# Eight batches of attention and adapters on one core: the loop over the first seven batches written out

## The reference

```python
x = x + attn0(prev=x, self=f)            # 16 heads of 32: q from f, k and v from x, plus one "self" score per row
x = x + softmax((x + e[stage]) @ f.T) @ f # one head over all 512 values
h = relu(x @ W1[lang] + b1[lang])
x = x + norm(x + h @ W2[lang] + b2[lang]) * gamma[lang] + beta[lang]
x = x + (x @ A[r].T) @ B[r].T + lang_embed[r]
```

## Time and profile before

| | before |
|---|---|
| median of three runs | 1429.83 us (1429.33 to 1430.75) |
| span of the profiled execution | 1427.7 us |
| PE busy | 1320.6 us, 92% |
| DVE busy | 930.6 us, 65% |
| ACT busy | 880.7 us, 62% |
| POOL busy | 430.4 us, 30% |
| chain that ended last | PE 61%, ACT 13%, DVE 12%, issue 11%, DMA 1%, POOL 1% |

### The profile page before, as it was taken

One profiled execution on the slowest core, in us unless ns is written; L12 is line 12 of the kernel. 1 busy time (PEld: TensorE's weight loads), 2 busy tenths in 40 slices (PEclk: granted clock), 3 DMA queues, 4 the chain that ended last, 5 costly groups with the idle time before them and its releaser, 6 DMA issues.

```text
span 1427.7 us, 22882 instructions
## 1 busy us (share of the span) xinstructions
PE 1320.6 (92%) x7009; PEld 560.8 (39%) x7009; DVE 930.6 (65%) x1594; ACT 880.7 (62%) x1853; POOL 430.4 (30%) x372
## 2 busy tenths in 40 slices
PE   4799999899998999889998899989999999999995
PEld 1332354324633255332553235432354324533253
DVE  6386458864688546975569654896458864688444
ACT  2398536974378834877448764587536874378731
POOL 5331026310443105331064201651026310443114
PEclk8899999999999999999999999999999999999996
DMA  4213012130120302212021301213012130120200
GB/s 159 70 45 99 1 36 69 38 107 1 53 71 28 99 15 59 62 65 52 31 56 49 115 1 31 74 38 108 1 41 65 45 100 1 54 73 24 69 1 30
DMA packets 62204, 76.26 MB, mean 53 GB/s; under 512 B 14378, under 2 KB 35174, under 8 KB 62062
## 3 DMA queue, kind: packets, MB, share of 16 engines
q1 hardware_dynamic: 62062, 74.54, 18.4%
HBM read 40.81 MB, written 8.40 MB: 34 GB/s over the span
## 4 chain that ended last, share of the span: by engine, by line
PE 61%; ACT 13%; DVE 12%; issue 11%; DMA 1%; POOL 1%; DVEq 0%; ACTq 0%; SPq 0%; POOLq 0%
PE bank L441 22%; PE banks L441 12%; DVE nmx L974 7%; PE bank L1319 7%; PE banks L1303 6%; ACT banks L734 6%; PE bank L1164 5%; ACT big L786 5%; PE banks L1237 3%; PE bank L1266 2%; PE bank L1329 1%; PE bank L1271 1%; PE bank L1293 1%; DVE y L1020 1%; PE bank L1224 1%
## 5 line engine op out<-in xcount | busy, mean ns | idle before, releaser
L734 ACT ACTIVATE banks<-banks,nmx 128x512 f32<-128x512 f32 x512 | 340.5, 671 | 55.8 <-DVE nmx L974 53.1
L974 DVE TENSOR_REDUCE nmx<-banks 128x1 f32<-128x512 f32 x512 | 325.9, 683 | 69.7 <-PE banks L1237 67.9
L786 ACT ACTIVATE big<-banks 128x1024 f32<-128x1024 f32 x256 | 247.9, 1021 | 64.5 <-PE banks L1303 49.7
L441 PE MATMUL bank<-fT,w_hi 128*128 128x512 f16 x768 | 244.0, 379 | 0.8
L1237 PE MATMUL banks<-KQ 97*128 97x512 f16 x512 | 154.1, 382 | 39.5 <-ACT banks L734 36.9
L516 POOL TENSOR_TENSOR big<-x,b2r 128x512 f32<-128x512 f32 x32 | 40.6, 1268 | 438.6 <-DVE x L909 397.5
L1303 PE MATMUL banks<-KQ 98*128 98x512 f16 x512 | 146.7, 396 | 23.5 <-ACT big L786 18.6
L441 PE MATMUL bank<-fT,w_lo 128*128 128x512 f16 x384 | 145.5, 379 | 0.0
L1319 PE MATMUL bank<-big,V 128*32 128x512 f32 x1024 | 142.2, 629 | 0.0
L477 POOL TENSOR_TENSOR half<-qk,ones 128x512 f16<-128x512 f32 x64 | 66.6, 1040 | 240.0 <-ACT qk L716 240.0
L441 PEld LDWEIGHTS bank<-fT,w_hi 128*128 128x128 f16 x768 | 74.7, 97 | 90.9 <-issue 11.9
(11 more groups left out here) (142 smaller groups left out, 1987.6 us busy)
## 6 DMA issues: line engine op xcount, KB each, us to landing
KQ<-half SPq DMA_DIRECT2D x384, 64.0 KB, 2.0
tiles_in<-in_x_dram SPq DMA_DIRECT2D x32, 256.0 KB, 7.1
tiles_in<-in_fside_BxSxS_dram SPq DMA_DIRECT2D x32, 256.0 KB, 2.7
x<-in_x_dram SPq DMA_DIRECT2D x8, 1024.0 KB, 5.4
out_dram<-x SPq DMA_DIRECT2D x32, 256.0 KB, 2.1
w<-in_L_cond_W_dram SPq DMA_DIRECT2D x16, 256.0 KB, 4.6
b2r<-in_L_cond_b_dram SPq DMA_DIRECT2D x8, 256.0 KB, 4.5
gr<-in_L_cond_gamma_dram SPq DMA_DIRECT2D x8, 256.0 KB, 5.3
```

The lines of the kernel that those rows point to most:

```text
L441: mm = eng.matmul(out_ap, pairs[n][0], pairs[n][1], start=(first and n == 0), stop=(last and n == len(pairs) - 1))
L734: ins = eng.activation(bank(step, i)[:, j % 2, :], bank(step, i)[:, j % 2, :], ACT.Exp, bias=nmx[:, t, h:h + 1], accum_out=esum[:, t, h:h ...
L786: eng.activation(big[:, n % 2, 2 * u:2 * u + 2, :], bank(step)[:, :, :], ACT.Exp).then_inc(read(step), 1)
L974: eng.tensor_reduce(nmx[:, t, h:h + 1], bank(step, i)[:, j % 2, :], AX_X, ALU.max, negate=True).then_inc(max_done, 1)
```

## The change

The five loops become Python loops, so each engine gets seven copies of the pass. The loop register, the branch and the instructions that work out counts and addresses go away. The order of the other instructions stays as it was on every engine. All five places of the diff read alike; two of them:

```diff
@@ POOL, L541 @@
-            with eng.Fori(0, B - 1) as i:
+            for i in range(B - 1):
                 add_bo(i)
                 mid(True, True, i)
             add_bo(B - 1)
```

## The result

The changed kernel takes 1403.95 us (median of four runs, 1402.62 to 1405.11) against 1429.58 us: 0.9818 of the time before, with a 95% interval of 0.9806 to 0.983. That is 25.6 us less, where 22.6 were predicted; 1407.2 us was the prediction, 1402.5 to 1411 us its range. Run once more, beside the kernel before on one other chip, it took 1403.04 us against 1430.71: 27.7 us less. The profiled execution took 1404.92 us with a span of 1402.9 us, 24.8 us under that of before.

A forecast was written before the change was run, and what follows sets the result against it. PE was taken as the bound (busy 92%), made to wait behind ACT's branch back. Terms -22.90 + 0.31 + 0 = -22.6 us took the 1427.7 us span to 1405.1, plus 2.1 for the runs' median: 1407.2 us, range 1402.5 to 1411.

The forecast's parts named there:

- Part 1: Start of attention, batches 1 to 6: without the six branches back, late exponential and lower PE clock go, saving 22.90 us.
- Part 2: Branches on PE, DVE, POOL and SP: hidden or already counted in the attention windows, so nothing is added.
- rival C: Start of attention: something else, such as shift rows or SP's loads, is late instead; 1429 to 1430 us, chance 0.05.
- Part 3: Attention: waits by constants add a semaphore instruction, five steps of 0.06 us; pass 0 loses 0.31 us.
- Part 4: Register instructions in layer1 and mid: taken as 0, between 3.5 us gained and 2.1 us lost.
- rival A: Mid: all 0.5 us a pass of DVE's wait at L964 is gained too, giving 1403.7 us; chance 0.09.
- the main case: Whole kernel: the summed terms hold, giving 1405 to 1409.5 us; chance 0.75.
- Part 5: Instruction fetch: seven written-out copies need no more code brought in than the loop does now; cost 0.
- Rival D: Instruction stream falls behind at block ends, 2.7 us a stop; at two a pass 1445 us, slower; chance 0.05.
- Rival B: Start of attention: PE's clock falls all the same, only the late exponential goes; 1417.0 us, chance 0.06.

The follow-up runs named there:

- ACT's loop alone: The changed kernel with only ACT's loop put back, the other four engines written out: 1427.63 us, 0.9971 of the kernel before.
- the request: Kernel before, all five loops kept, each asking for its loop's code ahead of the branch: 1415.00 us; with ACT alone so, others written out: 1408.09 us.
- PE kept at work: Changed kernel with ACT's loop back and 12 extra matmuls on PE while it waits for ACT's first exponential, passes 1 to 6: 1415.05 us.
- both places of ACT's loop: Kernel before, five loops, DVE's loop starting at place 0 of a code block, ACT's at place 0 (1428.21 us) or 64 (1429.43 us).

## Why the prediction was right

**Part 1, the branch back.** Right in size, -22.9 us in the attention of batches 1 to 6 for 22.90 forecast, and right in cause. ACT's branch alone carries it (ACT's loop alone). It is the wait for code: a packet of instructions comes within each of ACT's six silences, and with the request neither packets nor silences are left. The prediction called the cause not shown by the trace; the DMA view of the kernel before shows it. It also said that 2.70 us agree in size with the Trainium skill's section Instruction fetch mechanics. That section gives no duration, so no size could agree or differ. That the clock is half of the excess is now shown and not inferred: with PE busy in the hole the clock stays up and 2.0 us a pass come back. My split, 2.50 us for the late exponential, was near the 2.2 us that this run shows for the wait (the six attentions take 38.18 us in the mean, against 35.97).

**Part 2, the other branches.** Right: DVE's long silence stays hidden, the shift rows were not late, and no new wait took the place of the old (rival C).

**Part 3, waits by constants.** Right in mechanism and size for the steps. The cause is the extra semaphore instruction, which held the wait that ends last; naming the waits in the other order removes it. For pass 0 I forecast 36.28 and it read 36.55 us in both profiles of the changed kernel. The further 0.27 us are one stop: at 141.11 us ACT is silent 0.32 us between L347 and an exponential, where 0.04 us is usual. With the other order of waits it is gone; its cause is open.

**Part 4, layer1 and mid.** This is the term that was mis-sized. I took 0 between -3.5 and +2.1 us; it measured 7 x 0.69 = 4.8 us saved, beyond my upper end. The row that I had for the gain, 0.5 us of DVE at L964, was on the path: PE was 0.43 us earlier behind it. What misled me was to take layer1 as the nearest part in both forms. There PE has its inputs ready and DVE's sequencer is off the path; in mid PE waits for DVE's row maxima. So rival A, given 0.09, happened on top of the main case and went beyond its 3.5 us. The measured 1403.95 us is under the main case's 1405 us and lies in the range because the range took in A. There was luck in it too: the saving of 27.7 us, measured on one chip, taken from 1429.83 us gives 1402.1 us, just under the range. The late start and the 1.3 us of pass 5 hid part of the gain in the profiled execution.

**Part 5, more code.** Right, and more so: fewer packets, 99 for 142. Rival D did not occur: passes 1 to 6 without the dip agree to 0.03 us, with no unexplained stop of 2 us on PE or ACT; PE's longest idle stretch in a pass is 1.65 us, a wait for ACT's L734, at the same place each time. One argument for this was weaker than it looked: that two passes of the loop agree to 0.01 us shows that their block ends cost the same each time, and not that they cost nothing. The 0.40 us ahead of L964 were such a constant cost that hung on where the code lay.

**Rival B** fell: the clock is 1.00 in all eight attentions.

## What to carry to other kernels

A loop with a long body can pay for the branch back on the engine that others wait for at that moment (ACT was silent for 2.5 to 2.7 us; POOL with 103 rows a pass and SP with 149 for 0.2 to 0.3), and PE's clock can double the price; look for a silence behind the loop's line in the chain and for a packet of instructions within it in the DMA view, and compare the first pass with the later ones. If the profiled kernel has the same work once inside the loop and once outside, the windows give the forecast directly, but only for the stages that exist in both forms. Of two waits on one instruction, write the code so that the instruction itself carries the one that ends last; here that was the wait named first.

## What the hardware showed beyond this

- The request for the loop's code made the back edge nearly free (0.15 us on ACT) and the exit dear: 10.4 us with five engines, 4.6 us with ACT alone.
- PE's clock dips by itself in the middle of mid, with no stall ahead of it: once in seven passes of the profiled changed kernel (1.3 us), in none of its second profile, and once each in three of the other twelve (PE kept at work, both places of ACT's loop), always 94 us behind the end of an attention. Windows at the dip of pass 5 and at the same place in pass 3:

```profile
1086.00:1090.00 4.00, 3.04 (x9) 1.29 (x10) 3.86 (x12) 3.49 (x11) 0.00 (x0) 0.82 0.46 111
752.99:756.99 4.00, 3.04 (x12) 1.24 (x13) 3.86 (x12) 3.49 (x11) 0.00 (x0) 1.00 0.46 111
```

PE was busy 3.04 of 4 us in both, and only one has the dip. What decides is open. The 3.0 us between the two profiles of the changed kernel are such a dip (1.3) and a start that is 1.8 us later; for the spread of some 2.5 us between the other runs this is only argued.
